# Causal attention on one Trainium2 core: a section's maximum blocks in another order, two-block banks placed between one-block banks

## The chip, the cores and the metric

The kernel runs on one core of one Trainium2 chip. The metric is the device time of the whole program in microseconds. The kernel before took 1771.24 us, the median of three runs (1767.77 to 1772.6).

## What is computed

The reference is a small transformer on x of shape (4, 1024, 128), float32: a gated mixture of experts, a causal attention, the mixture again, a second mixture, a gated attention unit, and the second mixture once more, all with residual additions. The change touches the causal attention alone:

```python
q, k, v = heads(x @ w_in.T + b_in)            # 16 heads of 8
scores = einsum('bhqd,bhkd->bhqk', q * scale, k) + causal_bias
attn = softmax(scores, axis=-1)
out = einsum('bhqk,bhkd->bhqd', attn, v)
```

The softmax needs the largest score of each query before the exponentials are taken. The change alters in which order the pieces of that maximum are computed, and nothing else; the pieces are the same, and a maximum does not depend on their order.

## The kernel before, in words

**Phases.** The program is a row of phases: setup, a mixture phase, the attention phase (about 230 to 840 us of the profiled execution), three mixture phases with the gated unit between them. Only the attention phase (`phase_attention`, from line 851) changes.

**Sections.** The attention works in 16 sections, n = 0 to 15: a batch b = n // 4 and a group of four heads (HG = 4). Of each section two passes are made. The *maximum pass* computes scores with queries on the partitions, only to find each query's maximum. The *score pass* computes them again with keys on the partitions, subtracts the maximum (it was written as extra rows of q_st), takes the exponential on ScalarE (line 1159), masks the diagonal on GpSimd (line 1199) and multiplies with V on TensorE (line 1089, 16 matmul instructions for two units). The maximum pass of section n runs beside the score pass of section n - 1, interleaved on TensorE. In the profiled execution sections 6, 9, 10, 11 and 12 of the maximum pass begin at 435.7, 544.2, 579.8, 613.7 and 655.6 us, and section 13 at 687.4 us.

**Maximum blocks.** A block (t, c) is a query tile t (128 queries, t = 0 to 7) against the key half c (0 or 1, 512 keys each); the causal limit cuts its width to min(512, (t + 1) * 128 - c * 512). The tuple `MAXB` groups the twelve blocks of a head into nine PSUM banks of 512 columns: six banks hold one block of 512 columns, three hold two (128 + 384 columns twice, 256 + 256 once). Each bank is done for the four heads j = 0 to 3 in turn, so that a section has 36 banks. In this text bank number 4 * i + j is entry i of MAXB for head j. A block on the diagonal (c == t // 4) is *masked*: VectorE reads it with `tensor_tensor_reduce` against the causal mask (line 1284; in the profile a CUSTOM_DVE_ANT_0 and a DVE_READ_ACCUMULATOR2_ANT). A block below the diagonal is *plain*: one `tensor_reduce` of 512 columns (line 1286). The banks (4, 0), (5, 0), (6, 0), (7, 0) are plain; (3, 0) and (7, 1) are single masked blocks; the three two-block banks have two masked blocks each. TensorE fills a bank with one matmul per block (line 1051).

**The ring.** These banks, and those of the projections, of the turned maxima (`maxt`), of the turned outputs (`ot`, `ont`) and of the output projection (`wo`), go through three PSUM banks (RING = 3) in the order of `SLOT`. TensorE's `fill` waits until the bank's previous content, three slots earlier, has been drained; VectorE's last instruction on a bank tells that it is drained.

**The order.** `order()` writes the work of all engines out as one list sorted by a time in sections, and every engine walks this list in order, taking what is its own. The maximum banks of section n stand at n - 1.18 + 0.93 * (4 i + j) / 36, the score units at their share of columns, and the products with V ("pv") in pairs. `keys(n, h)`, the loads of the key half h into k_pad by SyncE (line 1240, four transfers of 48 KB), stand at n - 1.34 and n - 1.0; before them SyncE waits (line 1237) for the scores of section n - 2 that still read the buffer. `stats(b)` of the next batch (line 1252 and after, on VectorE) stands at n - 2.6, which falls between banks 22 and 23 of sections 2, 6 and 10.

**The wait for keys.** TensorE waits for the first key half at bank 0, and for the second at the first bank of entry `HALF1`, the first entry of MAXB that holds a block with c > 0 (line 869 and, in `peak`, line 1047).

Of the kernel before, what the change touches and what calls it, by code (L numbers as in the profile page):

```python
# [850 lines left out]
def phase_attention(nc, k, own, a, begun, lead):  # L851
# [12 lines left out]
    LOW, AGAIN = (1, 2), (2, 1)  # L864


    MAXB = (((3, 0),), ((4, 0),), ((5, 0),), ((6, 0),), ((7, 0),), ((0, 0), (2, 0)),
            ((7, 1),), ((4, 1), (6, 1)), ((1, 0), (5, 1)))
    HALF1 = next(i for i, parts in enumerate(MAXB) if any(c > 0 for _, c in parts))

    def width_of(t, c):
        return min(G, (t + 1) * P - c * G)
# [5 lines left out]
    def order():  # L878
# [10 lines left out]
        def put(t, *entry):  # L889
            timed.append((t, len(timed), entry))  # L890

        for n in range(SECTIONS):
# [12 lines left out]
            for h in range(HALF):  # L905
                put(n - 1.34 + 0.34 * h, "keys", n, h)
            for i in range(len(MAXB)):
                for j in range(HG):
                    put(n - 1.18 + 0.93 * (i * HG + j) / (len(MAXB) * HG), "max", n, j, i)
            put(n - 0.255, "neg", n)  # L910
# [26 lines left out]
    for entry in ORDER:  # L937
        if entry[0] in SMALL:
            if ("max", SECTIONS - 1, HG - 1, len(MAXB) - 1) in SLOT and n % RING == LENT:
                n += 1  # L940
# [4 lines left out]
    with ExitStack() as ctx:  # L945
# [63 lines left out]
        def _(pe):  # L1009
# [31 lines left out]
            def peak(n, j, i):  # L1041
# [5 lines left out]
                if i == HALF1 and j == 0:  # L1047
                    pe.wait_ge(k_in[n % 2][1], 16 * HG * (n // 2 + 1))
                for t, c in MAXB[i]:
                    width = width_of(t, c)  # L1050
# [196 lines left out]
        def _(dve):  # L1247
# [27 lines left out]
            def peak(n, j, i):  # L1275
# [3 lines left out]
                at = 0  # L1279
                for t, c in MAXB[i]:  # L1280
                    width = width_of(t, c)
# [494 lines left out]
def build(nc, a, out):  # L1776
    k = Core()
    lay, npack = pack_layout()
    with ExitStack() as ctx:
# [55 lines left out]
        def batch_ahead(stage, stack, beside_pass, unit, shift):  # L1835
# [15 lines left out]
            (0.70, "r5", g), (0.80, "cturn", g), (0.81, "rows", g), (0.90, "turn", g + 1), (0.91, "xh", g + 1),  # L1851
            (0.92, "xl", g + 1)]
        phase_attention(nc, k, att, a, begun, ffn0b)
        early.close()

# [111 lines left out]
```

## Time and profile before

| | |
|---|---|
| three runs | 1767.77, 1771.24, 1772.6 us |
| profiled execution, device time | 1770.8 us |
| its span in the trace | 1767.8 us |
| mean granted TensorE clock | 0.976 |
| TensorE busy | 1632.6 us, 92% of the span |
| VectorE busy | 1287.2 us, 73% |
| ScalarE busy | 1016.6 us, 58% |
| GpSimd busy | 775.2 us, 44% |

The span is the time from the first to the last instruction; the device time has 3.0 us more around it. A busy TensorE is not one at its peak: a matmul counts as busy from its issue until its modelled end, so that consecutive ones overlap, and a short wait between two of them may not show as idle time at all. It shows in the distance of their starts.

### The profile page before, as it was taken

Reading aid. Unit: us, or ns where it says so; the run is one execution under the profiler, and the core shown is the slowest. Engines: PE = TensorE matmul, PEld = TensorE weight load, DVE = VectorE, ACT = ScalarE, POOL = GpSimd, SP = SyncE. Lnnn points to the kernel's source line nnn. Section 1 sums busy time; section 2 is a strip of 40 time slices with the busy share of each in tenths; the row PEclk is TensorE's granted clock in tenths of the full one; section 3 lists DMA queues with packets and bytes.
Section 4 is the critical chain, followed back from the end, with each engine's and each line's share of the span. In section 5 each row is a group of like instructions: output and inputs, shape, how many; then the busy total and the mean of one; then the engine's idle time right before and its main releaser. Section 6 shows DMA issues by size and latency. Waiting matters only on the chain. (4 is left out here: it accounts for less than half of the span.)

```text
span 1767.8 us, 25916 instructions
## 1 busy us (share of the span) xinstructions
PE 1632.6 (92%) x8360; PEld 1159.7 (66%) x8360; DVE 1287.2 (73%) x3879; ACT 1016.6 (58%) x1718; POOL 775.2 (44%) x734
## 2 busy tenths in 40 slices
PE   5999889899899999997999989999998988999998
PEld 3777546555555555554777767777777876777776
DVE  6777578788778878862888767677666876777775
ACT  4666416565665666565666656555555645555554
POOL 2666601312311311121566656555573524555555
PEclk9999959999999999998999999999999998999999
DMA  4332121111111111100333341111110002111120
GB/s 149 98 98 94 54 36 33 20 23 23 25 30 21 26 21 34 20 11 14 109 118 121 103 135 55 48 49 48 55 43 1 1 2 94 56 55 60 55 95 19
DMA packets 58247, 95.01 MB, mean 54 GB/s; under 512 B 9313, under 2 KB 17121, under 8 KB 58113
## 3 DMA queue, kind: packets, MB, share of 16 engines
q1 hardware_dynamic: 56000, 91.07, 18.1%
q10 hardware_dynamic: 2112, 2.30, 0.4%
q8 instruction: 66, 1.08, 0.2%
q14 instruction: 69, 0.56, 0.1%
HBM read 76.76 MB, written 2.88 MB: 45 GB/s over the span
## 5 line engine op out<-in xcount | busy, mean ns | idle before, releaser
L697 DVE TENSOR_TENSOR big<-banks,big 128x512 f32<-128x512 f32 x384 | 264.6, 689 | 202.2 <-ACT banks L634 160.3
L1159 ACT ACTIVATE big<-banks 128x1024 f32<-128x1024 f32 (+3 forms) x384 | 301.5, 811 | 174.7 <-PE banks L1070 169.2
L634 ACT ACTIVATE banks<-banks 128x512 f32<-128x512 f32 x384 | 224.0, 583 | 276.5 <-PE banks L577 271.3
L707 DVE TENSOR_TENSOR big<-big,banks 128x512 f32<-128x512 f32 x400 | 274.9, 687 | 29.7 <-PE banks L580 15.8
L1051 PE MATMUL banks<-arena 128*128 128x512 f32 (+3 forms) x768 | 250.6, 403 | 27.5 <-DVE att_mx L1284 15.2
L1199 POOL TENSOR_SCALAR_AFFINE_SELECT big<-big 128x512 f32<-128x512 f32 x128 | 81.2, 635 | 403.7 <-ACT big L1159 403.7
L1284 DVE CUSTOM_DVE_ANT_0 banks<-banks,att_mask 128x128 f32<-128x128 f32 (+3 forms) x512 | 234.0, 523 | 29.2 <-PE banks L1051 28.5
L667 POOL TENSOR_TENSOR ffn1b_hid_l<-big,ffn1b_hid_h 128x512 fp32r<-128x512 f32 x128 | 165.4, 1292 | 128.6 <-ACT ffn1b_hid_h L639 128.6
L1070 PE MATMUL banks<-arena 128*128 128x512 f32 (+3 forms) x768 | 207.4, 356 | 12.0 <-ACT big L1159 12.0
L667 POOL TENSOR_TENSOR ffn1a_hid_l<-big,ffn1a_hid_h 128x512 fp32r<-128x512 f32 x128 | 165.3, 1292 | 116.6 <-ACT ffn1a_hid_h L639 116.6
L577 PE MATMUL banks<-xh,arena 128*128 128x512 f32 x512 | 208.0, 406 | 8.2 <-PEq L1450 6.8
L1051 PEld LDWEIGHTS banks<-arena 128*128 128x128 f32 x768 | 135.5, 198 | 116.1 <-DVE att_mx L1284 48.3
L580 PE MATMUL banks<-xh,arena 128*128 128x512 f32 x512 | 202.7, 396 | 0.0
L1286 DVE TENSOR_REDUCE att_mx<-banks 128x1 f32<-128x512 f32 x256 | 161.0, 683 | 26.0 <-PE banks L1051 25.4
L1070 PEld LDWEIGHTS banks<-arena 128*128 128x128 f32 x768 | 133.9, 191 | 40.9 <-ACT big L1159 26.3
L1089 PE MATMUL banks<-big,att_v_aug 128*32 128x512 f32 (+3 forms) x1536 | 145.0, 495 | 0.6 <-POOL big L1199 0.6
L667 POOL TENSOR_TENSOR ffn0a_hid_l<-big,ffn0a_hid_h 128x512 fp32r<-128x512 f32 x72 | 92.7, 1288 | 75.4 <-ACT ffn0a_hid_h L639 75.2
L667 POOL TENSOR_TENSOR ffn0b_hid_l<-big,ffn0b_hid_h 128x512 fp32r<-128x512 f32 x72 | 93.0, 1291 | 62.5 <-ACT ffn0b_hid_h L639 61.8
L577 PEld LDWEIGHTS banks<-xh,arena 128*128 128x128 f32 x512 | 96.9, 189 | 29.4 <-issue 8.9
L580 PEld LDWEIGHTS banks<-xh,arena 128*128 128x128 f32 x512 | 96.7, 189 | 22.1
L580 PE MATMUL banks<-xl,arena 128*128 128x512 f32 x256 | 101.5, 397 | 0.0
L577 PE MATMUL banks<-xl,arena 128*128 128x512 f32 x256 | 100.8, 394 | 0.0
(256 smaller groups left out, 3171.6 us busy)
## 6 DMA issues: line engine op xcount, KB each, us to landing
big<-weight_rows SPq DMA_DIRECT2D x256, 128.0 KB, 2.9
big<-weight_rows SPq DMA_DIRECT2D x128, 256.0 KB, 4.1
arena<-att_parts SPq DMA_DIRECT2D x16, 384.0 KB
arena<-att_parts SPq DMA_DIRECT2D x128, 48.0 KB
w_raw<-in_ffn_w_dram SPq DMA_DIRECT2D x12, 256.0 KB, 3.0
out_dram<-x SPq DMA_DIRECT2D x8, 256.0 KB, 2.3
setup_raw<-in_ffn_w_dram SPq DMA_DIRECT2D x3, 576.0 KB, 7.1
gau_angle<-in_consts_dram SPq DMA_DIRECT2D x2, 512.0 KB, 7.3
```

The lines of the kernel that those rows point to most:

```text
L577: mm = pe.matmul(gate_ps[:, num % NB, :], w[:, ws], xx[:, g % 2, :], start=m == 0, stop=m == 2)
L580: mm = pe.matmul(up_ps[:, num % NB, :], w[:, ws], xx[:, g % 2, :], start=m == 0, stop=m == 2)
L634: act.activation(gate if c < NSCALED else sil, gate, ACT.Silu).then_inc(silu_done, 1)
L667: pool.tensor_tensor(hid_l[:, num % NH, :], hid[:, num % NH, :], hid_h[:, num % NH, :].bitcast(F32), ALU.subtract).then_inc(low_cut, 1)
L697: dve.tensor_tensor(scl[:, num % 2, :], gate_ps[:, num % NB, :], share[:, c // PER, :], ALU.mult)\
L707: dve.tensor_tensor(hid[:, num % NH, :], scl[:, num % 2, :] if c < NSCALED else sil, up_ps[:, num % NB, :], ALU.mult).then_inc(hidden, 1)
L1051: mm = pe.matmul(bank[:, at:at + width], q_st[:, n % 3, t * P:(t + 1) * P], k_pad[:, n % 2, j, c * G:c * G + width], start=True, stop=True ...
L1070: mm = pe.matmul(score_ps[:, pair, h, 0:c], k_pad[:, n % 2, 2 * pair + h, kb * P:(kb + 1) * P], q_st[:, n % 3, (qg + 1) * G - c:(qg + 1) * ...
L1089: mm = pe.matmul(o_ps[32 * j:32 * j + 32, G - c:G], v_aug[:, b % 2, kb, at:at + 32], probs[:, unit % NPROB, j, 0:c], start=kb == 0, stop=k ...
L1159: act.activation(probs[:, unit % NPROB, 2 * pair:2 * pair + 2, 0:c], score_ps[:, pair, :, 0:c], ACT.Exp, scale=SCALE).then_inc(exped, 1)
L1284: ins = dve.tensor_tensor_reduce(now, now, mask[:, G - width:G], 1.0, -3e38, ALU.add, ALU.max, best)
L1286: ins = dve.tensor_reduce(best, now, AX.X, ALU.max)
```

## The change

The nine entries of MAXB stand in another order:

```diff
-    MAXB = (((3, 0),), ((4, 0),), ((5, 0),), ((6, 0),), ((7, 0),), ((0, 0), (2, 0)),
-            ((7, 1),), ((4, 1), (6, 1)), ((1, 0), (5, 1)))
+    MAXB = (((3, 0),), ((0, 0), (2, 0)), ((4, 0),), ((5, 0),), ((4, 1), (6, 1)), ((6, 0),), ((7, 1),), ((7, 0),),
+            ((1, 0), (5, 1)))
     HALF1 = next(i for i, parts in enumerate(MAXB) if any(c > 0 for _, c in parts))
```

| entry i | banks | before | after |
|---|---|---|---|
| 0 | 0 to 3 | masked 512 | masked 512 |
| 1 | 4 to 7 | plain 512 | two blocks, 128 + 384 |
| 2 | 8 to 11 | plain 512 | plain 512 |
| 3 | 12 to 15 | plain 512 | plain 512 |
| 4 | 16 to 19 | plain 512 | two blocks, 128 + 384 |
| 5 | 20 to 23 | two blocks, 128 + 384 | plain 512 |
| 6 | 24 to 27 | masked 512 | masked 512 |
| 7 | 28 to 31 | two blocks, 128 + 384 | plain 512 |
| 8 | 32 to 35 | two blocks, 256 + 256 | two blocks, 256 + 256 |

`HALF1` follows from the tuple: it was 6 (bank 24) and becomes 4 (bank 16). The times at which the entries stand in the order do not change, nor does anything else.

## Rows read from the trace of the kernel before

**Rows 1.** The page: span, busy times, granted clock in 40 slices.
```profile
span 1767.8 us, 25916 instructions
PE 1632.6 (92%) x8360; PEld 1159.7 (66%) x8360; DVE 1287.2 (73%) x3879; ACT 1016.6 (58%) x1718; POOL 775.2 (44%) x734
...
PEclk9999959999999999998999999999999998999999
```

**Rows 2.** Windows: stretch and length; PE, PEld, DVE, ACT, POOL busy; PEclk; DMA, GB/s.
```profile
435.70:470.40 34.70, 31.64 (x204) 19.59 (x202) 28.75 (x105) 20.23 (x27) 12.97 (x17) 0.95 0.14 26
...
544.20:579.80 35.60, 33.86 (x225) 20.88 (x226) 29.96 (x93) 21.20 (x29) 7.63 (x10) 1.00 0.14 25
579.80:613.70 33.90, 30.71 (x203) 18.34 (x201) 28.52 (x105) 20.21 (x27) 12.97 (x17) 1.00 0.15 26
613.70:655.60 41.90, 37.37 (x239) 23.37 (x235) 30.87 (x93) 25.91 (x37) 7.42 (x12) 1.00 0.13 21
655.60:687.40 31.80, 30.86 (x205) 18.37 (x201) 26.31 (x87) 20.24 (x27) 5.08 (x8) 1.00 0.17 28
...
234.80:258.10 23.30, 23.29 (x48) 12.86 (x48) 22.48 (x73) 0.00 (x0) 0.00 (x0) 0.50 0.20 34
```

**Rows 3.** Waits, 260 to 800 us: total, times, longest.
```profile
PEld banks L1051 <- DVE att_mx L1284: 42.2, 87, 2.7
```

**Rows 4.** Timeline of VectorE, section 12: start, duration, engine, line, instruction, count.
```profile
670.09 1.88 DVE L1286 TENSOR_REDUCE att_mx<-banks 128x1 f32<-128x512 f32 x3
671.88 0.29 DVE L1284 CUSTOM_DVE_ANT_0 banks<-banks,att_mask 128x128 f32<-128x128 f32 x1
...
672.61 0.33 DVE L1284 CUSTOM_DVE_ANT_0 banks<-banks,att_mask 128x128 f32<-128x128 f32 x1
...
675.08 0.73 DVE L1284 CUSTOM_DVE_ANT_0 banks<-banks,att_mask 128x512 f32<-128x512 f32 x1
...
675.73 0.73 DVE L1284 CUSTOM_DVE_ANT_0 banks<-banks,att_mask 128x512 f32<-128x512 f32 x1
```

**Rows 5.** Timelines of TensorE (PE matmul, PEld weight load), section 12.
```profile
662.77 0.19 PEld L1051 LDWEIGHTS banks<-arena 128*128 128x128 f32 x1 [0.29 <-DVE att_mx L1286]
...
666.68 0.40 PE L1051 MATMUL banks<-arena 128*128 128x512 f32 x1
...
670.54 0.40 PE L1051 MATMUL banks<-arena 128*128 128x512 f32 x1
...
670.83 0.19 PEld L1051 LDWEIGHTS banks<-arena 128*128 128x128 f32 x1 [0.32 <-DVE att_mx L1286]
...
672.02 0.19 PEld L1051 LDWEIGHTS banks<-arena 128*128 128x128 f32 x1
...
672.97 0.86 PE L1089 MATMUL banks<-big,att_v_aug 128*32 128x256 f32 x16
673.76 0.78 PE L1051 MATMUL banks<-arena 128*128 128x128 f32 x3
...
675.28 0.19 PEld L1051 LDWEIGHTS banks<-arena 128*128 128x128 f32 x1 [0.47 <-DVE att_mx L1284]
...
676.58 0.19 PEld L1051 LDWEIGHTS banks<-arena 128*128 128x128 f32 x1 [0.46 <-DVE att_mx L1284]
```

**Rows 6.** TensorE at the end of section 12, then SyncE's key loads.
```profile
682.79 0.50 PE L1051 MATMUL banks<-arena 128*128 128x256 f32 x2 [0.23 <-DVE att_mx L1284]
...
687.44 0.47 PE L1051 MATMUL banks<-arena 128*128 128x512 f32 x1
...
661.31 2.89 SPq L1240 DMA_DIRECT2D arena<-att_parts  x4
...
682.39 2.83 SPq L1240 DMA_DIRECT2D arena<-att_parts  x4
```

**Rows 7.** The statistics of the next batch: VectorE and TensorE in section 10.
```profile
598.31 1.63 DVE L1252 BATCH_NORM_STATS2 att_st<-x 128x6 f32<-128x128 f32 x8
...
601.66 0.50 PE L1051 MATMUL banks<-arena 128*128 128x512 f32 x1 [2.27 <-DVE att_mx L1284]
```

## Prediction

> **What bounds the kernel now.** I read the page first: over the whole span TensorE is busy 92% and VectorE 73%, and the granted clock is full but for a few slices [rows 1]. An average says little of one stage, so next the windows from the start of one maximum pass to the next [rows 2]. There are four kinds of section. A plain one (12) takes 31.8 us; one with the output projection beside it (9) 35.6; one with the next batch's statistics (10) 33.9; one with the next batch's projections (11) 41.9. In all of them TensorE is busy nearly throughout and VectorE about five sixths of the time or less. The kinds return every four sections, so a saving in a plain section is had in six (1, 4, 8, 12, 14, 15) and one of each other kind in three.
>
> Then the waits: TensorE's weight loads for maximum banks waited 42.2 us in 87 places for VectorE [rows 3]. That is all that a better order of the banks can take back, and weight loads partly overlap matmuls, so that it is an upper bound.
>
> Last the timelines of one plain section. VectorE does three plain banks in 1.88 us of which the last one's tail is 0.08, so **0.60 us a plain bank**; two-block banks begin 671.88 and 672.61, with the first one's tail in between, so **0.76** once they follow each other (0.73 here, 0.76 for the next); masked single ones begin 675.08 and 675.73, **0.65** [rows 4]. What TensorE issues for a bank is 512 columns in each case and takes the same to some 0.02 us. So VectorE's total is unchanged (24 banks of one, 12 of two blocks, per section) and only its timing beside TensorE moves.
>
> In the ring a bank may be filled 0.06 us after the bank three slots earlier is drained. In section 12 this binds at bank 10 (662.77, barely), 20 (670.83), 22 (672.02), 26 (675.28), 28 (676.58), 30, and 34 (682.79) [rows 5, 6]. Such a wait costs what the start is late, and another 0.10 as the weights were not loaded ahead: 0.16, 0.20, 0.31, 0.36 and 0.30 for banks 20, 22, 26, 28 and 30, 1.33 us together. This is what the new order could remove.
>
> **The change, part by part.** I walk one plain section with TensorE's distances as they are and VectorE's three durations; a time is "late" against the same bank before.
>
> *Entry 1 becomes two-block (banks 4 to 7).* The product with V lies between banks 5 and 6 and VectorE catches up in it; banks 6 and 7 end 0.09 late. Bank 10 must wait for bank 7: 0.10 us late.
>
> *Entry 4 becomes two-block (banks 16 to 19).* Bank 16 starts at 666.78. After V's product VectorE does the turned output and begins bank 17 at 670.19 (670.09 before [rows 4]). Banks 17, 18, 19 are drained at 671.05, 671.81, 672.57: late by 0.28, 0.44, 0.61. Bank 20 waits for 17 and starts 671.11 (0.28 late), bank 22 waits for 19 and starts 672.63 against 672.02 [rows 5], **0.61 late**.
>
> *Entry 5 becomes plain (20 to 23).* TensorE now leaves for V's product (672.97 before, 0.56 later now) and comes back for bank 23 at 674.32 against 673.76 [rows 5]. Before, the ring held two-block banks at this point, which kept VectorE busy until bank 23 came. Now it holds three of 0.60; VectorE ends at 674.37 and idles 0.5 us until bank 23 is full (674.87). Bank 23 is drained at 675.59, 0.37 late although it is shorter.
>
> *Entries 6 and 7 (24 to 31).* Bank 26 starts 675.65 against 675.28; bank 28 must wait for 25 and starts 676.95 against 676.58 [rows 5], both 0.37 late; bank 30 waits for 27, 0.38 late. So three of the five waits remain in smaller form, and 0.34 is left at V's second product. In the gap VectorE idled before too, so that the shorter banks 28 to 30 save nothing there.
>
> *Bank 31, and the end.* It is plain now, drained 0.16 late where TensorE is 0.34 late; bank 34 waits for it (682.79 before) and is 0.16 late. But the next section's first bank is held by the keys: SyncE issued them at 682.39 and bank 0 starts 687.44, 5.05 us later [rows 6]; the issue hangs on score units ahead of bank 33, where TensorE is 0.28 late. So the section passes on **+0.28 us**, and the 0.12 won at bank 34 is lost in this wait.
>
> *HALF1.* Bank 16 now waits for the second key half. Its transfers are issued from 661.31; if they take the 5.05 us of the others they are there at 666.36, and bank 16 started at 666.68 [rows 5, 6]: slack 0.3 us, 0.4 with the 0.10 lateness. I cost this at nothing; what hides it is the time TensorE spends on banks 8 to 15. Behind a late half would stand all of TensorE's queue, and VectorE and ScalarE with it. The queue of SyncE keeps its order.
>
> *The other kinds.* Statistics (2, 6, 10): up to bank 22 as above, then VectorE has 2.3 us of statistics from 598.31, and TensorE sits 2.27 us at bank 26 [rows 7]. VectorE is never idle there, so now the sums count: statistics begin 0.10 late, bank 23 is 0.19 shorter, bank 26 starts 0.09 earlier; the end is 0.13 earlier. Output projection (1 of 4: 5, 9, 13): late 0.44 at bank 22, regained by bank 30 as VectorE's row of work there contains one short bank in place of a long one: 0. Projections (3, 7, 11): the waits are few and other work lies between; about 0.1 late. Section 0 has no score pass beside it, runs 23.3 us at half the clock (1.2 GHz) with VectorE the bound [rows 2], and VectorE's sum is unchanged: 0. Where I had no own walk (projections) the bounds are those of the others, -0.13 and +0.28.
>
> *The clock.* In section 6 the mean granted clock is 0.95 and the section takes 34.7 us; section 10, the same work, has 1.00 and takes 33.9 [rows 2]. So one fall to the lower level (1.2 GHz) right behind the 2.3 us idle costs 0.8. The idle is now about 0.6 shorter, since TensorE comes to it later. Of two such falls (sections 2 and 6) I take one as gone: -0.8; bounds -1.6 and +0.8 (all three sections fall).
> The Trainium skill, "TensorE: Matmul & The Clock Gate", section "A second HAM failure mode: psum-queue depth-cycling", says that short idles of TensorE between groups, from cycling through PSUM banks, can make its clock swing between its levels. The trace does not agree for idles of this size: section 12 has all the waits above and a clock of 1.00 [rows 2]. By that rule the time would be the last rival's.
>
> *Sum.* Sections 4, 8, 12, 14: 4 x 0.28 = 1.1; section 15, with no keys behind it, 0.16, and section 1 about 0.2; output projection 0; statistics 3 x -0.13 = -0.4; projections 3 x 0.1 = 0.3; clock -0.8. Together **+0.6 us**. The profiled execution took 1770.8, 0.4 under the median of 1771.24, so the forecast is 1771.8. Each step of the walk is good to some 0.1 and a section ends on three or four of them, say 0.35: 15 x 0.35 = 5, own range 1767 to 1777.
>
> **The rivals.**
>
> *The waits simply go (faster).* If two-block banks among single ones let VectorE keep up, and the waits at banks 20 to 30 vanish: 6 x 1.33 = 8.0 in plain sections, 3.0 in three with statistics, 1.5 and 0.9 in the rest, less 15 x 0.1 at bank 10: 11.9, so 1759; half of it gives 1765. For it: between 670 and 680 us VectorE has 0.6 us less to do. Against it: bank 17 now leads in a row of long banks right behind V's product, when the ring is empty. Chance 0.20.
>
> *The 0.61 us at bank 22 is kept (slower).* One mechanism: three long banks right behind V's product starve TensorE, and nothing is regained by bank 31. It decides if VectorE's idle behind bank 22 is over the 0.5 us that I found. Price 6 x 0.6, 3 x 0.6 and 3 x 0.3 in the plain, output and projection sections = 6.3 us, in place of my 1.4: 1771.2 + 6.3 = 1778. Chance 0.12.
>
> *The keys' second half.* If it lands 0.3 us later than its slack in each of 15 sections: 4.5 us, 1776; with 0.5, 1779. For it: a slack of 0.3 with nothing else to cover. Against: its trigger moves with TensorE. Chance 0.05.
>
> *The clock.* If spread-out waits bring a fall at 0.8 us in each of 15 sections: 12 us, 1784. Against it the 1.00 of sections 9 to 12. Chance 0.03.
>
> **How the numbers follow.** A measurement of this kernel can tell about 0.3%, 5.3 us, from no change: faster means under 1766, slower over 1776.5. The forecast (0.60) lies within; so do the weakest forms of the key rival, which take 0.02 to it. Faster 0.20, same 0.62, slower 0.18. The range takes in my own one, the upper half of the faster rival and the slower one up to 1779: 1763 to 1779.
>
> **What would show it.** In a plain section after: a wait at bank 10 of 0.1 more; TensorE's start of bank 20 and 22 later by 0.3 and 0.6 than before, counted from bank 0; VectorE idle about 0.5 us just before bank 23, where it was not; waits at banks 26, 28, 30 still there but shorter; section 12 as long as before to 0.3 us. TensorE's idle in sections 2, 6, 10 near 1.7 us in place of 2.27. I am wrong if a plain section is a full 0.7 us shorter, or if bank 16 is released by a transfer.

## The result and the profile after

Over 20 runs of each the kernel before takes 1768.62 us in the median (1763.8 to 1772.78) and the changed one 1773.11 us (1768.9 to 1777.09). The ratio is 1.003, with a 95% interval of 1.002 to 1.0039: **slower by 0.3%, some 3.5 to 6.9 us**. The forecast was 0.6 us more than before, 1771.8 us, with a range of 1763 to 1779. The time lies in the range, the mechanism was the one forecast, and its size was too small: the difference is 4.5 us where 0.6 was forecast. That the forecast of 1771.8 comes within 1.3 us of 1773.11 is luck. It was built on 1771.24, the median of three runs, and twenty runs give 1768.62.

The page of the changed kernel, the line of busy times that answers to [rows 1]:

```profile
PE 1639.5 (92%) x8360; PEld 1159.2 (65%) x8360; DVE 1286.4 (73%) x3879; ACT 1017.8 (57%) x1718; POOL 775.1 (44%) x734
```

VectorE has the same work (1286.4 us against 1287.2), as it should: nothing was added. So the page can't say where the time went. The windows can. These are sections 6, 10, 11 and 12 of the changed kernel, from first bank to first bank, with the columns of [rows 2]:

```profile
433.80:468.02 34.22, 31.21 (x201) 18.19 (x201) 28.51 (x105) 20.32 (x27) 12.97 (x17) 1.00 0.15 26
...
578.20:613.40 35.20, 32.40 (x201) 18.78 (x202) 28.54 (x105) 20.31 (x27) 12.96 (x17) 0.95 0.14 25
613.40:655.86 42.46, 37.84 (x235) 23.29 (x236) 30.79 (x93) 26.00 (x37) 7.42 (x12) 1.00 0.12 21
655.86:688.17 32.31, 30.96 (x201) 18.17 (x202) 26.23 (x87) 20.34 (x27) 5.08 (x8) 1.00 0.17 28
```

Against [rows 2] the plain section 12 takes **32.31 us in place of 31.80**, the one with the output projection (section 9, 542.50 to 578.20) 35.70 for 35.60, the one with projections 42.46 for 41.90, and one with statistics and a full clock 34.22 (section 6) for 33.90 (section 10 before). In the other two sections with projections (3 and 7) the difference is 0.2, so that section 11 is the largest of its kind. Summed by kind: 5 x 0.5 plain, 0.3 for section 15, 3 x 0.3 with statistics, 0.2 + 0.2 + 0.6 with projections, about 0.2 with the output projection: 4.9 us, the size of the measured 4.5. Taken directly, from the first bank of section 1 to the last of section 15, the two traces differ by 4.2 us. So nothing outside the attention phase is needed to explain the difference. The phases outside it, whose code is the same, took 2.5 us less ahead of it and 3.1 us more behind it in this execution: a pair of traces tells of a section, and only the medians tell of the program.

Now the timeline of TensorE and VectorE in section 12. To compare with [rows 4, 5] take 0.21 off each time, since bank 0 starts at 655.86 here and at 655.65 before.

```profile
661.98 0.45 PE L1051 MATMUL banks<-arena 128*128 128x128 f32 x2
...
663.39 0.19 PEld L1051 LDWEIGHTS banks<-arena 128*128 128x128 f32 x1 [0.47 <-DVE att_mx L1284]
...
671.60 0.19 PEld L1051 LDWEIGHTS banks<-arena 128*128 128x128 f32 x1 [0.17 <-DVE att_mx L1284]
...
673.13 0.50 PE L1051 MATMUL banks<-arena 128*128 128x512 f32 x1 [0.27 <-DVE att_mx L1284]
...
674.81 0.50 PE L1051 MATMUL banks<-arena 128*128 128x512 f32 x1
...
676.09 0.19 PEld L1051 LDWEIGHTS banks<-arena 128*128 128x128 f32 x1 [0.29 <-DVE att_mx L1286]
...
677.40 0.50 PE L1051 MATMUL banks<-arena 128*128 128x512 f32 x1
```

| bank | before | after, less 0.21 | late | forecast late |
|---|---|---|---|---|
| 10 | 662.77 | 663.18 | 0.41 | 0.10 |
| 20 | 670.83 | 671.39 | 0.56 | 0.28 |
| 22 | 672.02 | 672.92 | 0.90 | 0.61 |
| 23 | 673.76 | 674.60 | 0.84 | 0.56 |
| 26 | 675.28 | 675.88 | 0.60 | 0.37 |
| 28 | 676.58 | 677.19 | 0.61 | 0.37 |
| 0 of section 13 | 687.44 | 687.96 | 0.52 | 0.28 |

The reader is to see one thing: the last two columns differ by 0.31 at bank 10, and by 0.23 to 0.29 at every bank after it. The walk was near in each later step of this section and lost 0.3 us at its first.

The waits at banks 26, 28 and 30 were forecast as "still there but shorter". Only bank 26's is shorter: the idle time of the weight load is 0.29 us for 0.47 at bank 26, 0.46 as before at bank 28, and 0.46 for 0.25 at bank 30. Between 260 and 800 us the weight loads of maximum banks waited 40.6 us for VectorE's masked banks (line 1284) and 15.4 for its plain ones (line 1286), 56.0 together. Before it was 42.2 and 10.0, 52.2 together.

VectorE's idle behind bank 22 was forecast as 0.5 us. Here it is, at bank 23:

```profile
672.93 1.88 DVE L1286 TENSOR_REDUCE att_mx<-banks 128x1 f32<-128x512 f32 x3
675.34 0.69 DVE L1286 TENSOR_REDUCE att_mx<-banks 128x1 f32<-128x512 f32 x1 [0.53 <-PE banks L1051]
```

VectorE does three short banks in 1.88 us and then waits 0.53 us for TensorE, which was away at V's product. Before, the three banks in the ring were long ones and VectorE had no such gap.

### The profile page after: what moved, and what is told of

The parts are those of the page before. It is cut to its first block and busy times, and to the rows that moved or that the text cites. A ratio compares the mean times of both kernels' runs of the same rounds, so it can differ in the third digit from the quotient of the medians.

```text
span 1772.5 us, 25916 instructions
## 1 busy us (share of the span) xinstructions
PE 1639.5 (92%) x8360; PEld 1159.2 (65%) x8360; DVE 1286.4 (73%) x3879; ACT 1017.8 (57%) x1718; POOL 775.1 (44%) x734
## 5 line engine op out<-in xcount | busy, mean ns | idle before, releaser
L1284 DVE CUSTOM_DVE_ANT_0 banks<-banks,att_mask 128x256 f32<-128x256 f32 (+3 forms) x512 | 236.1, 520 | 41.4 <-PE banks L1051 39.9
```

The source lines that it names most:

```text
L1284: ins = dve.tensor_tensor_reduce(now, now, mask[:, G - width:G], 1.0, -3e38, ALU.add, ALU.max, best)
```

## The experiments

**One move at a time.** The change moves two entries. Each was made alone.

```diff
-    MAXB = (((3, 0),), ((4, 0),), ((5, 0),), ((6, 0),), ((7, 0),), ((0, 0), (2, 0)),
+    MAXB = (((3, 0),), ((0, 0), (2, 0)), ((4, 0),), ((5, 0),), ((6, 0),), ((7, 0),),
             ((7, 1),), ((4, 1), (6, 1)), ((1, 0), (5, 1)))
```

> Only the first move of the change: the two-block entry (0,0)+(2,0) goes from entry 5 to entry 1; entry 7 and the wait for the second key half (bank 24) stay. Theory A (the loss comes from where long banks stand: a two-block bank costs TensorE about 0.05 us more, and behind V's product bank 10 waits for bank 7): bank 10 is 0.4 us late against before, counted from bank 0 of section 12, banks 17 to 20 are 0.4 late, VectorE idles before bank 23, and the plain section is about 0.15 to 0.4 us longer, the program 2 us slower. Rival B (the loss comes from the wait for the second key half at bank 16): no loss here, the section 31.8 us as before.

Measured: 1768.63 us against 1769.11, ratio 0.9995 (0.9981 to 1.0008), no difference that can be told; the 2 us of the expectation did not come. In the trace section 12 takes 31.91 us for 31.79 (the last digit before is from the starts of its first banks), a little less than the 0.15 expected at the least. The section and its bank 10:

```profile
656.47:688.38 31.91, 30.90 (x206) 18.19 (x202) 26.34 (x87) 20.33 (x27) 5.08 (x8) 1.00 0.17 28
...
664.00 0.19 PEld L1051 LDWEIGHTS banks<-arena 128*128 128x128 f32 x1 [0.47 <-DVE att_mx L1284]
```

It starts 7.53 us behind bank 0, exactly as in the changed kernel (663.39 - 655.86) and 0.41 later than before (662.77 - 655.65). So the whole 0.41 is entry 1's. But by the end only 0.12 of it is left: entry 5, plain now, lets TensorE catch up in the run of banks 20 to 26, where it had waited for VectorE before.

```diff
-    MAXB = (((3, 0),), ((4, 0),), ((5, 0),), ((6, 0),), ((7, 0),), ((0, 0), (2, 0)),
-            ((7, 1),), ((4, 1), (6, 1)), ((1, 0), (5, 1)))
+    MAXB = (((3, 0),), ((4, 0),), ((5, 0),), ((6, 0),), ((4, 1), (6, 1)), ((0, 0), (2, 0)),
+            ((7, 1),), ((7, 0),), ((1, 0), (5, 1)))
```

> Only the second move: the two-block entry (4,1)+(6,1) goes from entry 7 to entry 4, so that bank 16 waits for the second key half; entry 5 stays two-block. Theory A: nothing changes up to bank 16; then banks 17, 18, 19 are drained 0.2, 0.35, 0.5 us late, bank 22 starts 0.5 late, and 0.3 to 0.5 us is left at the next section's bank 0; the program 3 to 5 us slower. Rival B (keys): bank 16 itself starts late. Rival C (the two moves only cost together): section 31.8 us.

Measured: 1777.15 us, ratio 1.0046 (1.0028 to 1.0063), 8 us where 3 to 5 were expected. Section 12:

```profile
659.99:692.13 32.14, 30.88 (x201) 18.25 (x202) 26.26 (x87) 20.21 (x27) 5.07 (x8) 1.00 0.17 28
...
676.86 0.30 PEld L1051 LDWEIGHTS banks<-arena 128*128 128x128 f32 x2 [0.47 <-DVE att_mx L1284]
```

Bank 22 starts 16.87 us behind bank 0, 0.50 later than before, as expected; the section is 0.35 longer. With entry 1's 0.12 that makes 0.47 of the changed kernel's 0.52. **In section 12 the two moves add up**, each with its own cost, and entry 4 carries most. In program time the moves make -0.5 and 8 us, against 4.5 together; with intervals of -3.4 to 1.4 and 5 to 11 us this can't tell whether they add up. The whole program is slower than these section costs alone give. In this profiled execution the clock fell in all three sections with statistics (one of three with entry 1 alone), and two places come late by about a microsecond: bank 0 of section 4 and bank 16 of section 9. Both waited for keys. This is bank 16 of section 9:

```profile
557.46 0.53 PE L1051 MATMUL banks<-arena 128*128 128x128 f32 x2 [0.75 <-DMA arena<-att_parts]
```

SyncE issued this second key half at 551.17, so that bank 16 starts 6.3 us later; in the other plain sections of this trace it starts 5.4 us later. It is 0.93 late against before, and the section 1.1 us longer. This is rival B, in one section of fifteen. Bank 0 of section 4 starts 6.1 us behind the issue of the first half, where 5.0 is usual. That accounts for some 2 us of this one execution. Whether it also stands in the median of nine runs no trace shows, and the rest of the 8 us stays open.

**The wait for the second key half.** It moved from bank 24 to bank 16.

```diff
-    HALF1 = next(i for i, parts in enumerate(MAXB) if any(c > 0 for _, c in parts))
+    HALF1 = 4
```

> The order of before, but TensorE waits for the second key half at bank 16 in place of bank 24 (nothing else). Theory A: the half has landed by then, no difference: section 12 at 31.8 us and the program within 0.1%. Rival B (the key wait is the loss): section 12 about 0.5 us longer, the program 4 to 5 us slower.

Measured: 1770.95 us, ratio 1.001 (0.9996 to 1.0024), and section 12 takes 31.78 us (653.69 to 685.47), the 31.8 us of before. In this trace the wait makes bank 16 at most 0.1 us late in any of sections 1 to 15. In the trace of the changed kernel bank 16 starts 11.40 to 11.43 us behind bank 0 in all nine of sections 4 to 14 that have no projections: the half has landed there. So the wait is not the source of the 0.5 us. But it isn't without cost: four traced kernels wait for the half at bank 16, and in two of their sixty sections it came too late, by 0.9 us in the run above and by 0.5 us in section 6 of one below (the changed kernel with an early release). That would be some 0.35 us an execution, an estimate from these four traces; the interval of this run leaves room for up to 4 us.

**The wait for the first key half.** The forecast held that bank 0 of a section is released by the last of four key transfers and that TensorE's gain at bank 34 is lost there. To take the cause away, head 0's transfer counts on the queries' semaphore, and bank 0 waits for that alone:

```diff
-                    pe.wait_ge(q_in[n % 3], 16 * 2 * (n // 3 + 1))
-                    pe.wait_ge(k_in[n % 2][0], 16 * HG * (n // 2 + 1))
+                    pe.wait_ge(q_in[n % 3], 16 * 3 * (n // 3 + 1))
+                if i == 0 and j == 1:
+                    pe.wait_ge(k_in[n % 2][0], 16 * (HG - 1) * (n // 2 + 1))
...
-                                 parts[rows, 1, :, cut].bitcast(F32)).then_inc(k_in[n % 2][h], 16)
+                                 parts[rows, 1, :, cut].bitcast(F32)).then_inc(q_in[n % 3] if h == 0 and j == 0 else k_in[n % 2][h], 16)
```

(ScalarE's waits on the two counts follow.) On the order of before:

> The order of before, but bank 0 of a section waits only for the first head's keys (counted on the queries' semaphore), bank 1 for the other three. If bank 0 is held by the last of the four key transfers, its start comes about 0.2 us earlier in 12 of 15 sections: plain section 31.6 in place of 31.8, the program 2 to 3 us faster. If bank 0 is held by something else, no difference.

Measured: 1767.08 us, ratio 0.9995 (0.9984 to 1.0007); section 12 at 31.69 us. The wait was there, but of 0.1 us, not 0.2, and the 2 to 3 us of the program did not come. On the changed kernel:

> The changed kernel, with bank 0 waiting only for the first head's keys. Theory: section 13's bank 0 follows V's last product in 0.52 us in place of 0.78, the plain section takes 32.0 to 32.1 us against 32.3 of the changed kernel and 31.8 before; the program 2 to 3 us faster than the changed kernel, still 1 to 2 us slower than before. If bank 0 isn't held by the keys: 32.3 us.

Measured: 1771.09 us, ratio 1.0017 (1.0006 to 1.0029), 3.1 us slower than before where 1 to 2 were expected; section 12 at 32.08 us, as expected. The intervals of the ratios 1.0017 here and 1.003 of the changed kernel overlap, so that a gain of the whole program is not shown. Here are V's last product and bank 0 of section 13 behind it: the product before (its bank 0 is in [rows 6]), then both in the changed kernel, then both with the early release:

```profile
685.49 1.92 PE L1089 MATMUL banks<-big,att_v_aug 128*32 128x512 f32 x16
```

```profile
686.06 1.93 PE L1089 MATMUL banks<-big,att_v_aug 128*32 128x512 f32 x16
688.17 0.47 PE L1051 MATMUL banks<-arena 128*128 128x512 f32 x1 [0.18 <-DMA arena<-att_parts]
```

```profile
686.14 1.93 PE L1090 MATMUL banks<-big,att_v_aug 128*32 128x512 f32 x16
687.99 0.50 PE L1052 MATMUL banks<-arena 128*128 128x512 f32 x1
```

2.11 us become 1.85. The changed kernel's row names the transfer as what it waited for. Before, the same distance is 1.95 (685.49 to 687.44). The early release takes 0.23 off a section of the changed kernel and 0.10 off one of before. So of the 0.52 us that the change adds to a plain section, 0.13 stands in this place (the distance says 0.16), and 0.39 is there without it (32.08 against 31.69). TensorE has the section's work done 0.4 late at bank 34, but the keys' issue was triggered when it was 0.5 late (683.10 against 682.39).

**A two-block bank turned round.** In the changed kernel TensorE is 0.05 us late for every two-block bank of entry 1. Its two matmuls take 0.06 and 0.23 us from start to start, 0.29 together, where the one of a plain bank takes 0.23. The reading to test: behind a short matmul the next weight load is not hidden whole. So the kernel before was run with the long block first.

```diff
-    MAXB = (((3, 0),), ((4, 0),), ((5, 0),), ((6, 0),), ((7, 0),), ((0, 0), (2, 0)),
-            ((7, 1),), ((4, 1), (6, 1)), ((1, 0), (5, 1)))
+    MAXB = (((3, 0),), ((4, 0),), ((5, 0),), ((6, 0),), ((7, 0),), ((2, 0), (0, 0)),
+            ((7, 1),), ((6, 1), (4, 1)), ((1, 0), (5, 1)))
```

> The order of before, but in the two-block banks of 128 and 384 columns the 384 are done first. In the changed kernel the matmul of 384 columns behind one of 128 took 0.23 us to the next where 384 columns alone need 0.18, so that a two-block bank costs TensorE 0.29 against 0.23 us. If the long matmul first hides the second weight load, each of 8 such banks in a section costs 0.05 less: the plain section 31.8 or up to 0.2 less. If the exposed load only moves behind the short matmul, 31.8.

Measured: ratio 1.0002 (0.9986 to 1.0017), section 12 at 31.67 us, 0.12 less than 31.79; in the plain sections 4, 8 and 14 it is 0.04 to 0.07 less. The starts say more. Bank 20 starts at 666.06; behind it come the score matmuls (line 1070) and bank 21:

```profile
666.41 0.68 PE L1070 MATMUL banks<-arena 128*128 128x512 f32 x2
666.92 0.33 PE L1051 MATMUL banks<-arena 128*128 128x384 f32 x1
```

Bank 20 now takes 0.35 us to the score matmuls, where it took 0.39 (670.83 to 671.22). But from there to bank 21 it takes 0.51 where it took 0.46 (671.22 to 671.68), so that the whole is 0.86 against 0.85. The late weight load follows the short matmul wherever that stands: it moved behind it, as the last sentence of the expectation says, and TensorE gains nothing. What section 12 gains comes at bank 23: it is full some 0.05 us sooner behind its start, as its second matmul is the short one, and VectorE idles 0.02 us before it in place of 0.08.

**An order made by the mechanism.** If long banks belong into the ring when TensorE leaves for V's product, and short ones behind it, then the twelve two-block banks should stand at 5, 14 to 16, 20 to 22, 28 to 30 and 34, 35. The tuple is walked bank by bank:

```diff
+    KINDS = (0, 0, 0, 0, 2, 1, 2, 2, 2, 3, 3, 3, 3, 4, 1, 1, 1, 4, 4, 4, 7, 7, 7, 6, 5, 5, 5, 5, 7, 8, 8, 6, 6, 6, 8, 8)
+    SEQ = [(i, KINDS[:m].count(i)) for m, i in enumerate(KINDS)]
...
-            for i in range(len(MAXB)):
-                for j in range(HG):
-                    put(n - 1.18 + 0.93 * (i * HG + j) / (len(MAXB) * HG), "max", n, j, i)
+            for m, (i, j) in enumerate(SEQ):
+                put(n - 1.18 + 0.93 * m / len(SEQ), "max", n, j, i)
```

with MAXB as in the first experiment (1 is (0,0)+(2,0), 7 and 8 the other two, 6 is (7,1)).

> The 36 banks of a section in a hand-made order: the twelve two-block banks at 5, 14, 15, 16, 20, 21, 22, 28, 29, 30, 34, 35, that is in the ring when TensorE leaves for a product with V; masked single ones at 0 to 3, 23, 31, 32, 33; plain ones elsewhere, above all at 17 to 19 and 24 to 27. Theory A (long banks belong in front of a gap in TensorE's filling, short ones behind it): bank 26, 28 and 30 wait less than before, section 12 takes 31.3 to 31.6 us against 31.8, the program 3 to 6 us faster than before. Rival C (only how many long banks stand in a row matters, or the sum): 31.8 us, no difference.

Measured: 1765.9 us, ratio 0.9987 (0.9974 to 1.0), about 2 us less where 3 to 6 were expected, and at the edge of no difference. Section 12, and the weight loads of banks 24 to 30 that waited for VectorE. There are two; before there were three, of 0.47, 0.46 ([rows 5]) and, at bank 30, 0.25:

```profile
654.26:685.63 31.37, 30.48 (x201) 18.40 (x202) 26.52 (x87) 20.34 (x27) 5.08 (x8) 1.00 0.17 29
...
673.84 0.19 PEld L1052 LDWEIGHTS banks<-arena 128*128 128x128 f32 x1 [0.35 <-DVE att_mx L1285]
...
674.98 0.30 PEld L1052 LDWEIGHTS banks<-arena 128*128 128x128 f32 x2 [0.37 <-DVE att_mx L1287]
```

31.37 us, 0.42 less than before and 0.94 less than changed, with the same banks. Part of the program's shortfall may be chance: in this trace bank 0 of section 7 waited 1.29 us for late keys. With the early release of bank 0:

> The hand-made order, and bank 0 waiting only for the first head's keys. If the time won inside the section would be lost at bank 0 behind the keys (in the changed kernel bank 0 came 0.78 us after V's last product began its last group, 0.60 before, 0.52 with no wait for keys), this is another 0.1 to 0.3 us a section faster than the hand-made order alone; if not, the same as that.

Section 12 takes 31.23 us (652.37 to 683.60). The program takes **1762.89 us, ratio 0.9964 (0.9951 to 0.9977)**: 0.4% faster than before, with the same work.

## Why the prediction was right or wrong

**Right: the place and the mechanism.** The largest step of the cost lies in banks 17 to 23, where long banks follow V's product and short ones are in the ring at the next. Bank 22 was forecast 0.51 later than bank 16's lateness would make it (0.61 less 0.10), and came 0.52 later (0.90 less 0.38). The idle of VectorE was forecast at 0.5 and is 0.53. The regain by bank 28 was 0.24 forecast, 0.29 measured. Bank 16 was not released by a transfer. The order made from the same mechanism went the other way, as it should.

**Wrong: the first step, "bank 10 must wait for bank 7: 0.10 us late".** It was 0.41. Two errors are in it. The text took a bank's issue on TensorE as "the same to some 0.02 us"; a two-block bank takes 0.05 to 0.06 more, so that bank 7 starts 0.17 late. And VectorE was reckoned at its pace of 0.76 us a bank, while at banks 6 and 7 it comes from idle. There it waits for the second block's matmul (0.06 more) and takes 0.87 us where a plain bank took 0.70. So bank 7 was forecast drained 0.09 late and is 0.17 + 0.06 + 0.17 = 0.40 late. The entry 1 experiment shows this 0.41 alone, and that alone it comes down to 0.12 by the section's end; in the change entry 4 puts its own 0.5 on top before the same regain. All terms behind it were built on it, so that a plain section was forecast at 0.28 and costs 0.52. That section 12 would be as long as before to 0.3 us was a sign named in the prediction, and it failed.

**Wrong in size: statistics sections.** Forecast 0.13 earlier, measured 0.3 later (34.22 against 33.90). The sum there was that VectorE is never idle and only its total counts. That holds, but the total begins where VectorE reaches the statistics. Counted from bank 0 this was 18.48 us before (598.31) and is 19.02 now (452.86 in section 6), 0.54 later where 0.10 was forecast. Bank 35 is 0.14 late at the end, and the wait for keys makes 0.32 of it at the next bank 0.

**Wrong in size: projections.** They had no walk of their own. Forecast 0.1 each, measured 0.2, 0.2 and 0.5. Of the 3.9 us between forecast and result the plain sections with 1 and 15 make about 1.4, statistics 1.3, projections 0.6, output projection 0.2 and the clock 0.8, by the traces (4.3 together).

**Wrong: the upper bound of what an order can take back.** The 42.2 us of [rows 3] were read as all waits of weight loads for VectorE. They are those that a masked bank ended (line 1284); 10.0 us in 35 places ended with a plain one (line 1286). No term of the sum used it.

**Half right: the keys at bank 0.** That the gain at bank 34 is lost there is shown by the changed kernel's own row and by the early release. The expectations put the wait in the kernel before at 0.2 and it was 0.1.

**Wrong: the clock.** One of two falls was taken as gone. Both profiled executions have two of the three sections with statistics falling, in other sections (2 and 6 before, 2 and 10 after), although TensorE's idle went from 2.27 us to

```profile
600.25 0.50 PE L1051 MATMUL banks<-arena 128*128 128x512 f32 x1 [1.66 <-DVE att_mx L1286]
```

1.66, which had been forecast near 1.7. In traces of nearly the same order it fell in three of these sections (moved key wait), in two (early release on the order of before) and in none (blocks turned round). Each of these kernels has one trace, but within one trace sections with the same idle time fell and did not. So neither the order nor the idle time decides it here, and a term of the sum should not have been made of it: no run shows the 0.8 us that it took off. The last rival, that spread-out waits make the clock fall in each section, finds no support here: sections with all the waits above stay at 1.00.

**The rivals.** "The waits simply go" fell: bank 28 still waits for 0.46 us and bank 22 for more than before. "The 0.61 is kept" fell in its form, since 0.3 is regained, but its time, 1778 against 1771.2, was nearer to the measured difference of 4.5 us than the forecast's 0.6 was. The key half rival is not the source of the 0.5 us in a plain section, by its own experiment; as an occasional late landing of 0.5 to 0.9 us at bank 16 it is real, and its slack was 0.3 to 0.5 us. The chances gave "same" 0.62 and "slower" 0.18; with a ratio of 1.003, the 0.3% that the prediction set as the bound, the truth stands between the two.

## What to carry to other kernels

Where one engine fills a short ring and another drains it, what counts is how much draining time is in the ring at the moment the filler leaves for other work: long pieces in front of such a gap, short ones behind it. Spreading long pieces evenly is no aim in itself; here it cost 0.5 us in each plain section, and placing them before the gaps gained 0.4.

When such an order is walked, the first steps need the most care, since each later one inherits them: take a piece's cost for both engines, and its drain from idle as well as at pace. And a wait for a transfer that is triggered earlier in the same section passes on the lateness of its trigger, not that of the work just before it. To move such a wait to an earlier place may cost nothing in most sections and a microsecond in some, so look at every section of several traces and not at one.

## What the runs showed of the hardware

A matmul of 384 columns that follows one of 128 on other weights took 0.23 us to the next start, where 0.18 is usual for its columns. With the long one first the two took 0.18 and 0.06, and the matmuls behind them 0.05 more.

The key loads (four of 48 KB, the last issued 2.2 us behind the first) do not always take the same time. Bank 0 starts 5.0 us behind the first issue in most sections, but 5.8 in section 3 of the kernel before, 6.1 in section 4 with entry 4 alone, and 6.2 in section 7 of the hand-made order.

The fall of TensorE's clock behind an idle of 1.7 to 2.3 us at VectorE's statistics comes in some sections of one execution and not in others. In the changed kernel the idle was 1.66 us in section 10, which fell and took 35.20 us, and 1.65 in section 6, which did not fall and took 34.22.
